# Three activation tensors rounded to two-byte integers before they are turned, and the order of all steps planned anew

## What is computed

```python
h = rms_norm(x, g_pre)
a = sigmoid(bit_linear(h, w_a) + decay_bias); i = sigmoid(bit_linear(h, w_i)); v = bit_linear(h, w_v)
rec = scan(a, sqrt(clip(1 - a * a, 1e-8)) * (i * v))            # s[t] = a[t] * s[t-1] + input[t]
x1 = layernorm(x + (x + rec + bit_linear(silu(bit_linear(rms_norm(rec, g_post), w_gate)), w_down)))
x2 = layernorm(x1 + cross_attention(x1, ctx, mask))              # 16 heads of 16 channels, rope, 256 keys
out = layernorm(x2 + ffn(x2))                                    # 256 -> 1024 -> 1024 -> 256, weights +1 or -1

def bit_linear(x, w):                                            # integers times -1, 0, +1
    x_scale = clip(max(abs(x), axis=-1), 1e-5)
    x_q = clip(round(x / x_scale * 127.0), -128, 127)
    return einsum(x_q, w_q) * (w_scale * x_scale / 127.0)
```

## Times and profile before

| | us |
|---|---|
| median of 3 runs | 925.0 |
| lowest and highest run | 924.03, 1087.85 |
| the profiled execution | 922.5 |
| its span, first to last instruction | 920.3 |

### The profile page before, as it was taken

The page is one execution under the profiler, slowest core; times in us unless marked ns, Lnnn a source line. Parts: engine busy times, 40 slices in busy tenths (PEclk is TensorE's granted clock), DMA queues, the critical chain, the costliest instruction groups (busy, mean ns, idle before and its releaser), DMA issues.

```text
span 920.3 us, 17624 instructions
## 1 busy us (share of the span) xinstructions
PE 814.1 (88%) x6731; PEld 640.9 (70%) x6762; DVE 671.1 (73%) x1265; ACT 538.4 (59%) x896; POOL 277.6 (30%) x473
## 2 busy tenths in 40 slices
...
GB/s 287 0 64 64 41 87 2 127 2 126 13 92 49 59 81 41 100 2 139 2 120 20 88 52 61 79 42 98 3 138 2 120 19 65 53 54 63 1 13 23
DMA packets 52513, 57.42 MB, mean 62 GB/s; under 512 B 7856, under 2 KB 48848, under 8 KB 49360
## 3 DMA queue, kind: packets, MB, share of 16 engines
...
...
## 4 chain that ended last, share of the span: by engine, by line
PE 56%; DVE 22%; ACT 7%; DMA 6%; issue 5%; POOL 3%; SPq 0%; ACTq 0%; DVEq 0%; POOLq 0%
PE bankC L1067 15%; PE bankA L872 7%; PE slotB L990 6%; PE bankA L1003 6%; DVE nmax L1345 6%; PE bankA L937 6%; PE bankA L863 4%; DMA out<-x 4%; PE bankC L1052 4%; DVE h0l L1389 3%; PE bankC L1082 3%; PE slotB L971 2%; PE slotB L1022 2%; DVE st L1260 1%; DVE xg L1207 1%
## 5 line engine op out<-in xcount | busy, mean ns | idle before, releaser
L1067 PE MATMUL bankC<-h0h,w 128*128 128x256 f16 x1024 | 231.1, 272 | 6.6 <-DVE h0l L1389 6.6
L1067 PE MATMUL bankC<-h0l,w 128*128 128x256 f16 x1024 | 230.7, 272 | 0.0
L1345 DVE TENSOR_REDUCE nmax<-slotB 128x4 f32<-128x1024 f32 x128 | 154.1, 1218 | 8.0 <-PE slotB L971 7.0
L754 ACT ACTIVATE pr<-slotB 128x1024 f32<-128x1024 f32 x128 | 128.9, 1031 | 22.1 <-PE slotB L990 21.2
L1067 PEld LDWEIGHTS bankC<-h0h,w 128*128 128x128 f16 x1024 | 99.7, 97 | 22.5 <-issue 9.6
L1067 PEld LDWEIGHTS bankC<-h0l,w 128*128 128x128 f16 x1024 | 100.0, 98 | 11.5
L990 PE MATMUL slotB<-q_st,k_st 99*128 99x256 bf16 x512 | 78.4, 276 | 2.9 <-DMA q_st<-m_lo 2.2
L971 PE MATMUL slotB<-k_st,q_st 97*128 97x256 bf16 x512 | 76.7, 276 | 3.8 <-DVE nmax L1345 2.7
L651 ACT ACTIVATE rqT<-bankA,cst 128x512 bf16<-128x512 f32 x16 | 11.0, 687 | 111.8 <-PE bankA L863 111.8
L551 POOL TENSOR_SCALAR rstd<-mv 128x2 f32<-128x2 f32 x48 | 9.2, 191 | 219.5 <-DVE mv L1290 218.4
L779 ACT ACTIVATE h0h<-bankC 128x512 f16<-128x512 f32 x64 | 38.2, 597 | 60.9 <-PE bankC L1052 60.9
...
## 6 DMA issues: line engine op xcount, KB each, us to landing
...
```

Of the source, the lines that this page charges most:

```text
L754: act.activation(pr[i % 2][:, c, :, :].rearrange("p h s -> p (h s)"), slotB[ringB.slot(g, name)][:, :], ACT.Exp, scale=DH ** -0.5).then_in ...
L1067: ins = pe.matmul(bankC[ringC.slot(g, name)][:, e * T:(e + 1) * T], w_1[:, i // 2, (2 * m + e) * P:(2 * m + e + 1) * P], (h0h, h0l)[i % 2] ...
L1345: dve.tensor_reduce(nmax[:, hg * HG * NT + n:(hg + 1) * HG * NT:NT], slotB[ringB.slot(g, name)][:, :].rearrange("p (h s) -> p h s", s=S), ...
```

## The change

1. `round_tokens` gets a destination in two bytes (`xq`, `rq`, `gq`). After the two instructions that add `ROUND` it waits for them, waits that the batch before has turned its copy, and one further DVE instruction subtracts `ROUND` and writes two-byte values: 128x512 for `xq` and `rq`, 128x1024 for `gq`.
2. `turned` turns two-byte blocks with a two-byte identity into two-byte PSUM. The gate's eight turns fit one place of ring A, so `sqT0` and `sqT1` become one step `sqT`.
3. `integers` on ACT only copies: three reads a batch in place of four, of 128x512, 128x512 and 128x1024.
4. `scale` on POOL writes `xg` as soon as `round2` of the batch before is done, and no longer waits for the turn. `gate` on ACT waits for `q3` of the batch before.
5. `TIMES` and `BEGIN` are new, so the order changes on all engines.

```diff
-            def unround(g, name, dst):
+            def integers(g, name, dst, last):
+                if g >= 1:
+                    act.wait_ge(*ringA.filled(g - 1, last))
                 act.wait_ge(*ringA.filled(g, name))
-                act.activation(dst, bankA[ringA.slot(g, name)][:, :], ACT.Identity, bias=neg_round)\
+                act.activation(flat(dst), by_two_bytes(bankA[ringA.slot(g, name)])[:, 0:dst.shape[1] * T], ACT.Copy)\
                    .then_inc(ringA.free_sem(g, name), 1)
...
+            def turned(g, name, src):
+
+                take(g, ringA, name)
+                bank = by_two_bytes(bankA[ringA.slot(g, name)])
+                for c in range(src.shape[2] // P):
+                    for n in range(NT):
+                        ins = pe.transpose(bank[:, c * T + n * P:c * T + (n + 1) * P], src[:, n, c * P:(c + 1) * P],
+                                           ident_b[:, :])
+                ins.then_inc(ringA.full_sem(g, name), 1)
...
             def rqT_(g):
                 pe.wait_ge(*q2.at(g))
-                transposed(g, "rqT", xg)
+                turned(g, "rqT", rq)
...
-            def sqT_(g, k):
-                if k == 0:
-                    pe.wait_ge(*q3.at(g))
-                transposed(g, f"sqT{k}", sg[:, :, 2 * k * P:(2 * k + 2) * P])
+            def sqT_(g):
+                pe.wait_ge(*q3.at(g))
+                turned(g, "sqT", gq)
...
-            def round_tokens(g, src, factor, done):
+            def round_tokens(g, src, factor, dst, turn_step, done):
                 for n in range(NT):
-                    ins = dve.tensor_scalar(src[:, n, :], src[:, n, :], factor[:, n:n + 1], ROUND, ALU.mult, ALU.add)
-                ins.then_inc(done.sem, 1)
+                    own.mark(dve.tensor_scalar(src[:, n, :], src[:, n, :], factor[:, n:n + 1], ROUND, ALU.mult, ALU.add))
+                own.settle()
+                if g >= 1:
+                    dve.wait_ge(*ringA.filled(g - 1, turn_step))
+                dve.tensor_scalar(dst[:, :, :], src[:, :, :], -ROUND, None, ALU.add).then_inc(done.sem, 1)
...
                 if g >= 1:
-                    pool.wait_ge(*ringA.filled(g - 1, "rqT"))
+                    pool.wait_ge(*q2.at(g - 1))
                 pool.tensor_tensor(xg[:, :, :], x[g % 2][:, :, :], over_tokens(g_pre), ALU.mult).then_inc(xg_s.sem, 1)
```

More of the change, by code:

```diff
@@ L52 @@
 TIMES = """
[L53 to L76, removed]
+    w:s V-445.1 P-392.95 | w:m V-189.25 A-298.29 P-241.86 | w:a V-120.12 | w:iv V38.49 | w:g1 V-136.39 P4.63
+    w:g2 V-5.8 A0.93 P27.77 | w:gate V44.76 | w:down V63.91 | w:bv P23.92 A16.14 | w:bias P71.77 V90.24
@@ new lines @@
+    w:mask V53.22 S-109.29 | w:sgn V37 | w:k0 V38.67 | w:k2 V67.92 | w:k1.0 A80.91 | w:k1.1 A81.4 | w:k1.2 A89.4
+    w:k1.3 A89.72 | w:rope G13.79 P9.14 A5.86 | w:bqk P10.79 A22.85 | w:wk G30.61 | w:wq G66.68 | loadx S91.83
+    loadc S71.99 | scale A0 G13.05 V22.73 | stat1 G23.61 | round V37.51 | xqT P33.22 A39.79
+    iv0 P36.44 A45.81 V45.11 | iv1 P40.76 A48.02 V46.61 | a P36.06 A42.1 | aT P37.05 A44.03 | sq A53.27
+    ivT P45.5 V48.6 | cum V50.75 | recur V51.49 | rec P56.9 A67.24 V54.65 | max2 V54.82 | stat2 G64.55
@@ new lines @@
+    round2 V55.04 | rqT P64.33 A68.62 | gate0 P66.2 A70.25 V68.25 | gate1 P66.6 A72.27 V72.04 | stat3 G82.57
+    round3 V72.45 | sqT P72.03 A74.72 | down P74.11 V82.42 | bn V85.94 G98.24 | x1 V86.75 | kT P48.61 A58.75
+    v P50.02 A68.62 | rotk G63.75 | kp A67.47 V73.72 G96.11 | kput S64.59 | kget S77.58 | x1T P81.85 A85.11
+    xb G102.59 | q P84.76 V92.33 | rotq G113.75 V93.21 | qp A95.22 V93.67 | qput S94.27 | qget S99.64
+    score0 P106.44 V106.07 | score1 P111.32 V108.51 | score2 P112.12 V108.75 | score3 P116.52 V109.55
@@ new lines @@
+    score4 P117.12 V110.05 | score5 P119.5 V110.34 | score6 P120.1 V116.13 | score7 P121.08 V116.92
+    max P124.3 A127.21 V124.91 | maxrow S112.97 | exp0.0 P125.11 A128.49 | exp0.1 P126.73 A129.25 | pv0 P128.5
+    exp1.0 P127.93 A129.37 | exp1.1 P128.44 A132.57 | pv1 P134.29 A138.14 | exp2.0 P128.51 A137.15
+    exp2.1 P132.69 A138.04 | pv2 P138.26 | exp3.0 P136.78 A139.89 | exp3.1 P136.83 A143.58 | pv3 P140.21 A146.62
+    oTok P141.21 V147.35 | oT P144.54 A150.53 | wo P147.39 V150.29 | bn2 V151.29 G169.35 | x2 V155.71
```

48 lines of the change are left out of this document (30 added, 18 removed).

## The result

| | before | after |
|---|---|---|
| median, us | 924.5 (4 runs) | 940.1 (4 runs, 936.6 to 942.8) |
| ratio, 95% interval | 1 | 1.0185 [1.0146, 1.0224] |
| span of the profiled execution, us | 920.3 | 936.8 |
| granted TensorE clock over the span | 0.969 | 0.963 |

One of the runs before took 1087.85 us, in a slower state of the chip, and is left out of the ratio. The changed kernel is slower by 1.9%; the interval leaves open whether it is more or less than 2%. Forecast were 929 and a range from 908 to 947. In the steady part, 110 to 860 us, the clock is the full 2.4 GHz in both kernels (1.00 in the windows view), so the time did not go into the clock.

What follows compares the result with a forecast made beforehand. A chain handing over between PE and DVE was taken to bound the kernel. A -0.43 and B +0.65 gave +0.22 a batch, +3.3 over fifteen, +0.7 at the end: median 929 us, range 908 to 947.

Steps and rivals of the forecast that it cites:

- Part A: Stretch of a batch from DVE's split of x2 to PE's `exp0.0`: 25.09 to 24.7 us, counted as -0.43 a batch.
- (b): In part A, `max` goes ahead of one L1389 and one L1265 on DVE: -1.1 us a batch.
- (c): In part A, DVE's new two-byte pass in `round2`, covered by nothing: +0.53 us a batch.
- (d): In part A, POOL's `rotk` now meets DVE's two scans: +1.0 us a batch, ends 0 and 2.5.
- (a): In part A, L1260 no longer runs beside POOL's `xb`, which moves half a batch away: -0.86 us a batch.
- rival 3: Both scans wait for a whole POOL instruction, so (d) is 2.5: 951 us, slower; chance 15%.
- Part B: Stretch from `exp0.0` to DVE's next split of x2: 25.08 to 26.3 us, +0.65 a batch against the mean.
- The tail: One more part B at the end of the run, after the fifteen batches: +0.7 us.
- The start: Filling the pipeline: three open passes against cheaper turns and weights moved off ACT, taken as 0, from -3 to +3 us.
- Rivals 1: The scans miss `rotk` as `kb` comes later; (d) is 0 and PE's list decides part A: 915 us; chance 20%.
- 2: Scans miss `rotk`, and q's path is no later because ACT's exponentials pace part B: 904 us, faster; chance 8%.
- Rival 4: The two-byte turn is not cheaper; only the gate's eight in part B count: +6 us, 935; chance 7%.

Runs made afterwards that it cites:

- Experiment 4: Kernel before with only POOL's `xb` moved from behind `stat2` to behind `bn3` (its bias row made earlier): 910.3 us, ratio 0.9857.
- experiment 5: Changed kernel with DVE's row maxima put back behind gate1's product and the gate's turns and copy ahead of `exp0.0`: 949.8 us, ratio 1.0298.
- experiment 1: Changed kernel with the due times of the kernel before, so the two-byte path alone in the old order: 929.4 us, ratio 1.0064.
- experiment 11: Experiment 9's kernel with POOL's `rotk` also put back behind `stat2`, and ACT's `kp` with it: 913.8 us, ratio 0.9914 against the kernel before.
- experiment 12: Kernel before, turns in four bytes, with the due times of experiment 11: 919.1 us, ratio 0.9952.
- experiment 3: Changed kernel with POOL's `rotk` put back behind `stat2`, and ACT's piece of `kp` with it: 935.7 us, ratio 1.0129 against the kernel before.
- Experiment 6: Changed kernel with q's products on PE moved from behind `pv2` to between `exp3.0` and `exp3.1`: 942.1 us, ratio 1.0210 against the kernel before.
- experiment 9: Changed kernel with experiment 5's moves, and `down`, x1T, q and `exp3.1` put back too: 921.7 us, ratio 1.0002 against the kernel before.
- experiment 2: Kernel before, four-byte turns, with the due times of the changed kernel, so the new order alone: 944.6 us, ratio 1.0233.
- experiment 8: Experiment 4's kernel with ACT's `finish` moved earlier, between `exp3.0` and `exp3.1`: 913.8 us, ratio 0.9905 against the kernel before.

## Why the prediction came out as it did

The time of 940 is inside the range of 908 to 947 and 11 us above the figure, just outside the 919 to 939 that the prediction gave to its own forecast. The upper part of the wide range was there for scans that wait longer; the time came there for a reason that the prediction did not have. That it lies inside is luck. The prediction had a batch at 50.9 and called itself wrong in its core below 50.0 or above 52; it is 51.72.

**Part A was right in its sum, partly by luck.** Forecast were -0.43 us a batch in the mean; the traces give 25.89 - 25.32 = 0.57 less from x2's turns to `exp0.0` (0.58 from `xl`, where the prediction cut). The causes that it named are there, but (b) was taken 0.4 too high as a gain and (c) and (d) too high as costs, and these errors offset each other. Its terms:

- (a) L1260 no longer meets `xb`: 0.15 us in every batch, as said. Experiment 4 puts 0.69 a batch on it ahead of `exp0.0`, and 0.85 on the whole batch, where 0.86 was taken.
- (b) `max` ahead of two DVE instructions: forecast -1.1, measured -0.65 to -0.7 (experiment 5). The place won met the next wait: DVE idles before `m_lo` until ACT's `m_hi`, 5.6 us in 15 batches.
- (c) The pass of `round2`: 0.43 and 0.03 of waiting, 0.46 where 0.53 was taken. "In `round2` nothing covers it" was true of the old order (PE idle 0.94 until the pass ends, experiment 1) and false of the new one, where PE is busy 0.95 us past it, so that the pass does not delay `rqT` (experiments 11 and 12). The cheaper turns do shorten A there, against the prediction's "the saved turns are lost".
- (d) `rotk` meets the scans: they take 1.83 us for two in this timeline of DVE and 1.26 alone, so 0.57 more; this holds for 11 of the 16 pairs. The other five take 2.3 to 2.8 us. In the mean DVE loses 0.8 us a batch where 1.0 was taken; the path feels 0.4 in the median (experiments 3 and 11), and 0.6 a batch in the mean of experiment 11. The collision was read rightly from rows of other instructions, and its price on the path was taken too high. The rows of DVE and POOL, kernel after:

```profile
549.30 1.83 DVE L1258 TENSOR_TENSOR_SCAN rec<-av,u 128x256 f32<-128x256 f32 x2
...
548.25 1.27 POOL L578 TENSOR_TENSOR kt<-kb,turn 128x512 f32<-128x512 f32 x1 [5.66 <-ACT kb L717]
549.48 2.18 POOL L580 TENSOR_TENSOR kt<-kb,turn 128x256 f32<-128x256 f32 x2
```

POOL starts its rotation at 548.25, 3.4 us behind the start of A (544.87), the early end of the 3.4 to 8 that was forecast. POOL pays as well: L580 takes 2.18 us for two where it took 1.41. In this batch, instruction by instruction, the first scan ends at 550.07, the first L580 at 550.59, the second scan at 551.13 and the second L580 at 551.66, so they end in turn, 0.52 to 0.54 us apart. The Trainium skill (SBUF — State Buffer, Who interferes with whom) has the engine that issues first keep the shared ports for its whole instruction, while the other is blocked. The trace agrees: each ends about half a microsecond behind the end of the other's. The wait is for the rest of what is under way, here about 0.1 and 0.5 us, and not for 1.27 each as in rival 3.

**Part B was wrong, by about 1 us a batch.** Forecast was +0.65 against the mean; measured is 26.51 - 24.83 = 1.68 more from `exp0.0` to x2's turns. Two steps failed.

- *The cause of the late q.* The prediction had q end at T+13.1, since PE's list has three more items before it. q's result is with DVE at T+13.7 (531.57), near enough, but mostly for another cause. q starts 2.49 us later than before (T+11.71 against T+9.22). Experiment 6 takes it out from behind `exp3.1` and `pv2`; it then starts 0.76 us earlier, waits for x1T, and the batch does not get shorter. The other 1.73 us are x1T's. The chain gate, `down`, x1, x1T, q is late as a whole; `down` starts at T+4.0 where experiment 9 has T+1.3. The prediction costed the move of the maxima ahead of the gate as a pure gain in A. It is not free: `gq` comes 1.3 us later against `exp0.0`, so the gate's turns can't stand ahead of `exp0.0` without holding it up, and their copy and `down` come late with them. The new pass of `round3` was covered, as said: `gq` ends at 518.58 and PE reaches the turns at 519.15. The price of a move ahead of something was read only for what moves, and not for what is passed.
- *The parts behind oT.* oT starts at T+18.46 where 18.0 was forecast, and the -0.3 behind it did not come: from oT to `xl` it is 544.87 - 536.29 = 8.58 against 535.04 - 526.51 = 8.53. These two make this batch's B 0.76 longer than forecast (27.04 against 26.28). Most of the rest of the mean lies in two batches, the first and the one before the last, with 28.4 and 28.5.

One microsecond a batch is 15 us, and the range reached 18 us above the figure, so the time alone does not show that this step failed. The tail shows it again, as it holds one more B: +2.5 us, forecast +0.7. The start was -1.1, inside the -3 to +3.

**The rivals.** Rivals 1 and 2 (the scans miss `rotk`) fell with the scans' 1.14 us. Rival 3 fell since no pair lost more than 1.5 us and most lost 0.57; POOL's rotation starts 1.05 us before the first scan, and the rival asked for less than about 0.7. Rival 4 fell too: eight turns take 519.15 to 519.60, 0.056 each. The Trainium skill (TensorE: Matmul & The Clock Gate, Back-to-back issue gap) gives about 81 ns for such a product in a stream with weight loads. The trace does not agree: these eight come 0.056 us apart at full clock, with a load for each turn. What decided is a cause that the prediction did not have: the gate's chain slips behind `exp0.0`.

**Smaller points.** The pass over 128x1024 takes 0.69, forecast 0.8. The pass of `round` is covered, as said (DVE idle 1.86 before q's bias). The store no longer releases the instruction that writes x2: L1388 waits 16 times for PE and never for the DMA. The same holds in experiments 2, 3, 9, 11 and 12, all with the new tables, while with the old ones the wait stays even where `finish` is earlier (experiment 8). So the event came as forecast, and the cause given for it, the earlier `finish`, is not enough; which other move frees it is open.
